# Neighbour maxima over a sparse adjacency: the mask is transposed by DMA instead of by TensorE, and the work of a group is spread differently over its steps

## The chip, the cores and the metric

One core of a Trainium2 chip runs the whole program. The metric is the device time of one execution in microseconds (us), lower is better.

## What is computed

```python
# x: (8, 1024, 128) f32; adj: (8, 1024, 1024) int32, sparse; W: (256, 128); b: (128,)
h = maximum(layernorm(x), 0)
mask = adj != 0
idx = the first 25 set columns of each row of mask      # top_k of -column
agg = max over those neighbours of h[idx]               # and 0, where a row has <= 25
out = x + relu(concat([h, agg], -1) @ W + b)
```

## The kernel before

The 8 × 1024 rows are worked in 16 groups of 512 rows, two groups to a batch. A step of the loop handles one group g and, interleaved with it, prepares group g + 1 and g + 2. Columns are held in 8 classes k (column modulo 8), 128 columns on the partitions. For one group the work is:

- **Mask.** `load_adj` (L221) brings 512 rows of int32. Four signs, one for 128 rows each, make `mask` in bf16 (VectorE `make_mask` L636 for the first two groups, ScalarE `make_mask` L339 after that). `turn_mask` (L449) transposes it on TensorE, 8 blocks of 128×128 in each of 4 turns, into the two-bank PSUM ring, and ScalarE copies each turn to `mask_t` (`turned_mask`, L333).
- **Ranks.** `lower_sums` (L463, 8 matmuls) starts the running counts in the PSUM bank `side`. Then for k = 0 to 7: `prefix_sums` (L469, one matmul) finishes class k in `side`, ScalarE's `find_past` (L349) reads how far past 25 it is, and TensorE's `ranks` (L455, two matmuls) and ScalarE's `stage` (L344) give the rank of every neighbour. `prefix_sums` k waits for `find_past` k − 1.
- **Late neighbours.** `find_late` (L354) marks neighbours above rank 4 of their column block. Seven SyncE DMAs shift the marks by partition (`skew_late`, L233 and L235), `late_ranks` (L455, one or two matmuls a class) and `count` (L491, 8 narrow matmuls) rank them anew, and VectorE's `count_rounds` reads the count.
- **Picks.** A one-hot `hot` (L659, VectorE) times the features, in a high and a low part, fetches neighbours: a **use** is one `pick_pair` (four matmuls, L506 and L507) into one of two PSUM pairs, and one VectorE maximum, `take_pair` (L678). A group has 16 uses, 0 to 15. Uses 0 to 3 run at the end of the step before; ScalarE's `first_maxima` (L378) copies uses 0 and 1 out. Use n may start when take n − 2 has ended. After use 15 come R **late rounds** (R is 1 to 4, 42 in all), each two picks of eight matmuls, two maxima (L775) and two `late_hot` (L684).
- **End.** Two folding maxima (L782, L784), `project` on TensorE (L532, L534, L538) and `finish_group` on VectorE (L691). Group g ends while uses 0 to 3 of group g + 1 run.

The order is written out by hand. Three lists say with which use the preparatory matmuls are issued, right behind its picks, and ScalarE follows the same lists:

```python
LATE_WITH, PREFIX_WITH, RANK_WITH = spread_over(5, 8), spread_over(5, 12), spread_over(9, 13)
LATE_HOT_USES, COUNT_USE, MASK_USES = (10, 11), 9, (4, 9)
```

`LATE_WITH` and `PREFIX_WITH` give the uses of `late_ranks` and `prefix_sums`, `RANK_WITH` that of `ranks`; `count` follows the last `late_ranks`. `COUNT_USE` is the take behind which VectorE reads the count. `lower_sums` runs behind use 4.

New features are normalised once in two steps (odd steps): statistics on VectorE in uses 4 to 8, two passes on GpSimd (`normalize`), the two relu parts on ScalarE (`relu_parts`), the low part on GpSimd, then 14 shifting DMAs on SyncE (`skew_h`). In the start, before the loop, all of this runs once for batch 0, and the masks of groups 0 and 1 are made and turned.

## Time and profile before

| | |
|---|---|
| time, median of 3 runs | 699.37 us (698.42 to 699.73) |
| the profiled execution, its own time | 697.45 us |
| its span | 695.7 us |
| granted TensorE clock, mean | 0.993 |
| TensorE busy | 630.9 us, 91% of the span |
| VectorE busy | 613.7 us, 88% |
| ScalarE busy | 472.3 us, 68% |
| GpSimd busy | 50.3 us, 7% |
| DMA, share of 16 engines | 25.7% |
| VectorE waiting for picks before L678 | 36.0 us, 50 times |

Busy time of TensorE is the modelled length of matmuls that overlap in its pipeline (380 ns each where they start 216 ns apart), so a stretch of it is read from the starts in the timeline. A row of the timeline gives the start and length of an instruction (merged where equal ones follow, with xN), and in brackets how long its engine had been idle before it, and who ended that.

### The profile page before, as it was taken

What the parts mean: (1) busy time and instruction counts of PE and PEld (TensorE: products, weight loads), DVE (VectorE), ACT (ScalarE), POOL (GpSimd) and SP (SyncE); (2) the same over time, 40 slices, a digit from 0 to 9 for tenths busy, and PEclk for the clock granted to TensorE, in tenths of its full rate; (3) what the DMA queues carried; (4) which work ended last, traced back from release to release, by engine and by line L of the source; (5) the groups of instructions that cost most, each with busy time, mean ns of one, the idle gap of its engine ahead of it and who ended that gap; (6) DMA issues with size and microseconds to landing.
All of it is one profiled execution on the core that took longest, in us unless ns stands there. A gap on an engine that the chain in (4) does not pass through costs nothing.

```text
span 695.7 us, 10819 instructions
## 1 busy us (share of the span) xinstructions
PE 630.9 (91%) x3376; PEld 297.4 (43%) x3376; DVE 613.7 (88%) x813; ACT 472.3 (68%) x642; POOL 50.3 (7%) x41
## 2 busy tenths in 40 slices
PE   2479998999989999899999999899999999999976
PEld 2133443535445354443545344353535335353423
DVE  3368999899998999989998899989998899988997
ACT  2689478783777639775795947777497927959120
POOL 1300021000210002100030002100021000300000
PEclk9899999999999999999999999999999999999999
DMA  9520141510415103251303313151122411020100
GB/s 361 199 87 27 60 152 68 182 70 16 152 73 200 60 15 136 83 188 60 128 23 122 151 60 151 68 196 57 41 122 87 185 60 32 16 107 1 60 15 16
DMA packets 19127, 67.64 MB, mean 97 GB/s; under 512 B 4499, under 2 KB 7830, under 8 KB 16534
## 3 DMA queue, kind: packets, MB, share of 16 engines
q1 hardware_dynamic: 19094, 67.26, 25.7%
q8 instruction: 13, 0.21, 0.1%
q14 instruction: 20, 0.16, 0.1%
HBM read 42.08 MB, written 4.19 MB: 67 GB/s over the span
## 4 chain that ended last, share of the span: by engine, by line
PE 66%; DVE 16%; issue 10%; ACT 4%; DVEq 1%; DMA 1%; POOL 1%; ACTq 0%
PE picked L506 18%; PE picked L507 17%; PE ring L455 14%; DVE late_hot L684 4%; PE side L469 4%; PE ring L449 4%; DVE hot L659 4%; PE side L463 4%; DVE best L775 3%; DVE best L678 3%; PE final L534 2%; PE final L538 2%; PE final L491 1%; DMA adj_in<-in_adj_dram 1%; DVEq L771 1%
## 5 line engine op out<-in xcount | busy, mean ns | idle before, releaser
L678 DVE TENSOR_TENSOR best<-picked,best 128x1024 f32<-128x1024 f32 x224 | 270.5, 1218 | 38.2 <-PE picked L507 36.0
L506 PE MATMUL picked<-hot,h_hi 128*128 128x512 f16 x512 | 194.5, 380 | 15.0 <-DVE best L775 7.5
L507 PE MATMUL picked<-hot,h_lo 128*128 128x512 f16 x512 | 194.0, 379 | 0.0
L506 PE MATMUL picked<-late_hot,hi_skew 128*128 128x512 f16 x336 | 127.6, 380 | 13.1 <-DVE late_hot L684 8.2
L507 PE MATMUL picked<-late_hot,lo_skew 128*128 128x512 f16 x336 | 127.3, 379 | 0.0
L344 ACT ACTIVATE late_rank<-ring,late_bias 128x512 bf16<-128x512 f32 x128 | 81.4, 690 | 57.6 <-PE ring L455 57.6
L775 DVE TENSOR_TENSOR best<-picked,best 128x1024 f32<-128x1024 f32 x84 | 102.4, 1219 | 8.3 <-PE picked L507 8.2
L378 ACT COPY best<-picked 128x1024 f32<-128x1024 f32 x32 | 32.2, 1013 | 102.6 <-PE picked L507 102.6
L659 DVE TENSOR_SCALAR hot<-rank 128x4096 f16<-128x4096 bf16 x64 | 89.4, 1399 | 12.0 <-ACT rank L344 12.0
L349 ACT ACTIVATE past<-side,bias_cut 128x512 bf16<-128x512 f32 x128 | 88.3, 690 | 6.2 <-PE side L469 4.9
L344 ACT ACTIVATE rank<-ring,bias_big 128x512 bf16<-128x512 f32 x128 | 83.1, 692 | 5.2 <-PE ring L455 4.9
L684 DVE TENSOR_SCALAR late_hot<-late_rank,numbers 128x2048 f16<-128x2048 bf16 x116 | 86.1, 742 | 0.0
L506 PEld LDWEIGHTS picked<-hot,h_hi 128*128 128x128 f16 x512 | 50.1, 98 | 83.6 <-DVE best L775 14.9
L507 PEld LDWEIGHTS picked<-hot,h_lo 128*128 128x128 f16 x512 | 50.1, 98 | 48.4
L354 ACT ACTIVATE late<-rank,bias_late 128x1024 bf16<-128x1024 bf16 x64 | 68.2, 1137 | 0.0
L333 ACT ACTIVATE mask_t<-ring 128x1024 bf16<-128x1024 bf16 x64 | 62.2, 1023 | 4.8 <-PE ring L449 4.8
L506 PEld LDWEIGHTS picked<-late_hot,hi_skew 128*128 128x128 f16 x336 | 32.6, 97 | 72.0 <-DVE best L775 20.4
L339 ACT ACTIVATE mask<-adj_in 128x1024 bf16<-128x1024 int32 x56 | 57.4, 1050 | 2.8 <-issue 2.8
L469 PE MATMUL side<-mask_t,eye 128*128 128x512 bf16 x128 | 49.5, 387 | 9.4 <-ACT past L349 9.4
L449 PE MATMUL ring<-eye,mask 128*128 128x128 bf16 x512 | 41.0, 231 | 15.0 <-DVE mask L636 11.2
L309 POOL TENSOR_TENSOR h<-x_in,moments 128x1024 f32<-128x1024 f32 x8 | 15.6, 1949 | 500.7 <-DVE gain L655 500.7
L449 PEld LDWEIGHTS ring<-eye,mask 128*128 128x128 bf16 x512 | 40.1, 148 | 24.0 <-issue 11.5
(76 smaller groups left out, 562.1 us busy)
## 6 DMA issues: line engine op xcount, KB each, us to landing
adj_in<-in_adj_dram SPq DMA_DIRECT2D x16, 2048.0 KB, 7.7
late_skew<-late SPq DMA_DIRECT2D x32, 192.0 KB, 2.3
x_in<-in_x_dram SPq DMA_DIRECT2D x8, 512.0 KB, 8.5
xres<-in_x_dram SPq DMA_DIRECT2D x16, 256.0 KB, 7.8
late_skew<-late SPq DMA_DIRECT2D x16, 256.0 KB, 2.4
late_skew<-late SPq DMA_DIRECT2D x32, 128.0 KB, 2.0
out_dram<-xres SPq DMA_DIRECT2D x16, 256.0 KB, 2.0
late_skew<-late SPq DMA_DIRECT2D x32, 64.0 KB, 1.9
```

Source lines behind the costliest of these rows:

```text
L344: nc.scalar.activation(dst[:, k, :], ring[k % 2][:, :], ACT.Relu, bias=bias).then_inc(ring_read, 1)
L349: nc.scalar.activation(past[:, k, :], side[:, :], ACT.Relu, bias=bias_cut[:, 0:1]).then_inc(past_made, 1)
L354: nc.scalar.activation(late[:, 2 * p:2 * p + 2, :], rank[:, s, 2 * p:2 * p + 2, :], ACT.Sign, bias=bias_late[:, 0:1]).then_inc(late_made, 1)
L449: last = nc.tensor.transpose(ring16[n % 2][:, j, q * P:(q + 1) * P], mask[:, q, 2 * n + j::K], eye[:, :])
L455: last = nc.tensor.matmul(ring[k % 2][:, :], w[:, :], m, start=(i == 0), stop=(i == len(terms) - 1))
L469: nc.tensor.matmul(side[:, :], eye[:, :], mask_t[:, k, :], start=False, stop=True, skip_group_check=True).then_inc(prefix_written, 1)
L506: nc.tensor.matmul(dst, hi[:, slot, k, :], onehot, start=start, stop=False)
L507: return nc.tensor.matmul(dst, lo[:, slot, k, :], onehot, start=False, stop=stop)
L659: nc.vector.tensor_scalar(hot[:, (t - 1) % 3, :, :], rank[:, s, :, :], float(t), None, ALU.is_equal).then_inc(hot_made, 1)
L678: nc.vector.tensor_tensor(best[:, half, s, :, :], picked[s][:, :, :], best[:, half, s, :, :], ALU.max).then_inc(picked_read, 1)
L684: nc.vector.tensor_scalar(late_hot[:, part, :], late_rank[:, part, :], which, None, ALU.is_equal).then_inc(late_hot_made[i], 1)
L775: nc.vector.tensor_tensor(best[:, s, i, :, :], picked[i][:, :, :], best[:, s, i, :, :], ALU.max).then_inc(late_read[i], 1)
```

## The change

- **Mask.** The four signs of a group move to the end of a step on ScalarE, behind `first_maxima` (`make_masks`, changed L363), for group g + 3. They read the int32 rows with a step of 8 elements and write `mask` class by class. SyncE issues four DMA transposes a group (`turn_masks`, changed L257) into `mask_t`, which now has two halves. TensorE's 32 transposes and ScalarE's four copies of a group are gone.
- **Order on TensorE.** `lower_sums` for group g + 2 is issued behind `project`, ahead of use 4. The lists change: late ranks with uses 4 to 9, prefix sums with 4 to 11, ranks with 9 to 14. `count` follows use 9, VectorE reads it behind take 11, and makes the late one-hots behind takes 12 and 13.
- **Start.** The features load first and the first mask in four quarters with a semaphore each. VectorE makes only group 0's mask, and both relu parts and the low part of batch 0 (`first_parts`). ScalarE makes the masks of groups 1 and 2; those of group 1 stand ahead of `turned_h`, `find_late` and `first_maxima`. GpSimd's first normalisation waits for group 0's masks.

```diff
-    LATE_WITH, PREFIX_WITH, RANK_WITH = spread_over(5, 8), spread_over(5, 12), spread_over(9, 13)
-    LATE_HOT_USES, COUNT_USE, MASK_USES = (10, 11), 9, (4, 9)
+    LATE_WITH, PREFIX_WITH, RANK_WITH = spread_over(4, 9), spread_over(4, 11), spread_over(9, 14)
+    LATE_HOT_USES, COUNT_USE = (12, 13), 11
...
-        mask = sb("mask", [P, Q, N], BF16)
-        mask_t = sb("mask_t", [P, K, ROWS], BF16)
+        mask = sb("mask", [P, Q, K, P], BF16)
+        mask_t = sb("mask_t", [P, 2, K, ROWS], BF16)
...
+            def turn_masks(slot):
+                sp.reg_add(masks_due, masks_due, Q)
+                for q in range(Q):
+                    sp.wait_ge(mask_made, q + 1)
+                    if q == 0:
+                        sp.wait_ge(mask_made, masks_due)
+                    sp.dma_start_transpose(mask_t[:, slot, :, q * P:(q + 1) * P],
+                                           mask[:, q, :, :].rearrange("p k j -> p (k j)")).then_inc(mask_turned, 16)
...
             load_x(0)
+            for q in range(Q):
+                sp.dma_start(adj_in[:, 0, q * N:(q + 1) * N], adj_v[0][:, q * N:(q + 1) * N]).then_inc(adj_first[q], 16)
             load_adj(1, 1)
...
+            load_adj(2, 0)
+            turn_masks(1)
+            load_adj(3, 1)
             skew_h(0, 0)
             skew_late(0)
+            turn_masks(0)
             def step(it, u):
...
                         skew_h(batch_of(it, u + 1), ((u + 1) // PER_BATCH) % 2)
+                if not at_end(it, u, 3):
+                    turn_masks((u + 1) % 2)
                 sp.wait_ge(result_made, g + 2)
...
+            def make_masks(slot):
+                act.reg_add(turned_due, turned_due, TURNED)
+                act.reg_add(adj_due[slot], adj_due[slot], 16)
+                act.wait_ge(mask_turned, TURNED)
+                act.wait_ge(mask_turned, turned_due)
+                act.wait_ge(adj_loaded[slot], adj_due[slot])
+                for q in range(Q):
+                    counts = adj_in[:, slot, q * N:(q + 1) * N].bitcast(U32).rearrange("p (j k) -> p k j", k=K)
+                    nc.scalar.activation(mask[:, q, :, :], counts, ACT.Sign).then_inc(mask_made, 1)
...
-            stage(TURNS, K - 1, rank[:, 0], bias_big[:, 0:1])
+            stage(0, K - 1, rank[:, 0], bias_big[:, 0:1])
+            make_masks(1)
             turned_h(0, 0)
...
-                if not at_end(it, u, 2):
-                    for n in range(TURNS):
-                        turned_mask(at + TURN_AT, n)
+                if not at_end(it, u, 3):
+                    make_masks((u + 1) % 2)
...
-                    if use == PAIRS and more:
-                        lower_sums(at - TURNS)
...
-                if not at_end(it, u, 2):
-                    turn_mask(g + 2, at + TURN_AT, 0)
                 if more:
                     pick_pair(g + 1, 2, next_slot)
-                if not at_end(it, u, 2):
-                    turn_mask(g + 2, at + TURN_AT, 1)
-                if more:
-                    pick_pair(g + 1, 3, next_slot)
-                if not at_end(it, u, 2):
-                    turn_mask(g + 2, at + TURN_AT, 2)
-                    turn_mask(g + 2, at + TURN_AT, 3)
-                project(g, it, u, new_batch)
+                    pick_pair(g + 1, 3, next_slot)
+                project(g, it, u, new_batch)
+                if not at_end(it, u, 2):
+                    lower_sums(g + 2, u % 2)
...
+            def first_parts():
+                dve.wait_ge(normed_made, 1)
+                nc.vector.tensor_scalar(h_hi[:, 0, :, :], h32[:, :, :], 0.0, None, ALU.max).then_inc(h_made, 1)
+                dve.wait_ge(h_made, 1)
+                nc.vector.tensor_scalar(h32[:, :, :], h32[:, :, :], 0.0, None, ALU.max).then_inc(h_made, 1)
+                dve.wait_ge(h_made, 2)
+                nc.vector.tensor_tensor(h_lo[:, 0, :, :], h32[:, :, :], h_hi[:, 0, :, :], ALU.subtract).then_inc(lo_made, 1)
```

The order of instructions at the places that matter, as built. `ISA` and `REGISTER_ALU` are semaphore and register work and carry no busy time; line numbers of the change are those of its own file.

TensorE in a step, before, from the second half of `lower_sums` through the picks of use 5 to the late ranks of classes 0 and 1:

```order
L463 MATMUL side<-mask_t,before 128x512 x2
L462 REGISTER_ALU
L463 MATMUL side<-mask_t,before 128x512 x2
L518 REGISTER_ALU
L506 MATMUL picked<-hot,h_hi 128x512
L507 MATMUL picked<-hot,h_lo 128x512
L506 MATMUL picked<-hot,h_hi 128x512
L507 MATMUL picked<-hot,h_lo 128x512
L480 ISA
L455 MATMUL ring<-late_skew,half_w 128x512 x2
L455 MATMUL ring<-late_skew,half_ones 128x512
L469 MATMUL side<-mask_t,eye 128x512
```

And changed, the picks of use 4 and what follows them:

```order
L527 ISA
L515 MATMUL picked<-hot,h_hi 128x512
L516 MATMUL picked<-hot,h_lo 128x512
L515 MATMUL picked<-hot,h_hi 128x512
L516 MATMUL picked<-hot,h_lo 128x512
L489 ISA
L460 ISA
L465 MATMUL ring<-late_skew,half_w 128x512
L460 REGISTER_ALU
L465 MATMUL ring<-late_skew,half_w 128x512
L465 MATMUL ring<-late_skew,half_ones 128x512
L478 MATMUL side<-mask_t,eye 128x512
```

The lower sums (L463) stood behind use 4 and are now ahead of it, and the late ranks and the first prefix sum follow use 4 instead of use 5.

TensorE from `count` (L491) on, before; the ranks begin one use later, behind use 9:

```order
L491 MATMUL final<-late_skew,half_ones 32x512 x8
L468 REGISTER_ALU
L469 MATMUL side<-mask_t,eye 128x512
L518 REGISTER_ALU
L506 MATMUL picked<-hot,h_hi 128x512
L507 MATMUL picked<-hot,h_lo 128x512
L506 MATMUL picked<-hot,h_hi 128x512
L507 MATMUL picked<-hot,h_lo 128x512
L468 REGISTER_ALU
L469 MATMUL side<-mask_t,eye 128x512
L441 REGISTER_ALU
L455 MATMUL ring<-mask_t,rank_w 128x512
```

Changed, the tail of use 9:

```order
L465 MATMUL ring<-late_skew,half_w 128x512
L465 MATMUL ring<-late_skew,half_ones 128x512
L500 MATMUL final<-late_skew,half_ones 32x512 x8
L477 REGISTER_ALU
L478 MATMUL side<-mask_t,eye 128x512
L460 REGISTER_ALU
L465 MATMUL ring<-mask_t,rank_w 128x512
L465 MATMUL ring<-past,minus_w 128x512
L460 REGISTER_ALU
L465 MATMUL ring<-mask_t,rank_w 128x512
L465 MATMUL ring<-past,minus_w 128x512
L527 REGISTER_ALU
```

The count (L500), a prefix sum and the ranks of two classes stood behind two different uses and now stand behind one.

SyncE's queue in the start, before, up to the first of the 14 shifts of `skew_h` (L233, `hi_skew`):

```order
L221 DMA adj_in<-in_adj_dram 128x4096
L227 DMA x_in<-in_x_dram 128x1024
L221 DMA adj_in<-in_adj_dram 128x4096
L250 DMA w_in<-in_L_gnn_W_dram 128x2x128
L252 DMA bias_in<-in_L_gnn_b_dram 1x128 x3
L224 DMA xres<-in_x_dram 128x512
L221 DMA adj_in<-in_adj_dram 128x4096 x2
L233 DMA hi_skew<-h_hi 32x1024
```

Changed:

```order
L227 DMA x_in<-in_x_dram 128x1024
L262 DMA adj_in<-in_adj_dram 128x1024 x4
L221 DMA adj_in<-in_adj_dram 128x4096
L264 DMA w_in<-in_L_gnn_W_dram 128x2x128
L266 DMA bias_in<-in_L_gnn_b_dram 1x128 x3
L224 DMA xres<-in_x_dram 128x512
L271 DMA_TRANSPOSE mask_t<-mask 128x8x128 x4
L221 DMA adj_in<-in_adj_dram 128x4096
L252 REGISTER_ALU
L257 DMA_TRANSPOSE mask_t<-mask 128x8x128 x4
L221 DMA adj_in<-in_adj_dram 128x4096
L233 DMA hi_skew<-h_hi 32x1024
```

Eight transposes and a load now stand ahead of the shifts, four of them behind masks that ScalarE makes.

## Rows read from the trace of the kernel before

**Rows 1.** Groups by line and shape: busy, mean of one | idle before, releaser

```profile
L678 DVE TENSOR_TENSOR best<-picked,best 128x1024 f32<-128x1024 f32 x224 | 270.5, 1218 | 38.2 <-PE picked L507 36.0
...
L339 ACT ACTIVATE mask<-adj_in 128x1024 bf16<-128x1024 int32 x56 | 57.4, 1050 | 2.8 <-issue 2.8
L506 PEld LDWEIGHTS picked<-hot,h_hi 128*128 128x128 f16 x512 | 50.1, 98 | 83.6 <-DVE best L775 14.9 <-DVE best L678 14.7 <-issue 6.5
...
L449 PEld LDWEIGHTS ring<-eye,mask 128*128 128x128 bf16 x512 | 40.1, 148 | 24.0 <-issue 11.5 <-ACT mask_t L333 4.3
```

**Rows 2.** Timeline of VectorE, even steps 0 and 2: start, length, instruction, idle before

```profile
51.24 1.23 DVE L678 TENSOR_TENSOR best<-picked,best 128x1024 f32<-128x1024 f32 x1 [1.37 <-PE picked L507]
...
129.26 1.22 DVE L678 TENSOR_TENSOR best<-picked,best 128x1024 f32<-128x1024 f32 x1 [0.17 <-PE picked L507]
131.85 1.22 DVE L678 TENSOR_TENSOR best<-picked,best 128x1024 f32<-128x1024 f32 x1 [1.37 <-PE picked L507]
...
139.41 1.22 DVE L678 TENSOR_TENSOR best<-picked,best 128x1024 f32<-128x1024 f32 x1 [1.16 <-PE picked L507]
```

**Rows 3.** Timeline of VectorE, odd step 1, the same columns

```profile
92.65 1.22 DVE L678 TENSOR_TENSOR best<-picked,best 128x1024 f32<-128x1024 f32 x1 [0.59 <-PE picked L507]
...
100.42 1.23 DVE L678 TENSOR_TENSOR best<-picked,best 128x1024 f32<-128x1024 f32 x1 [0.39 <-PE picked L507]
101.56 0.68 DVE L664 TENSOR_REDUCE late_most<-final 128x1 f32<-128x512 f32 x1
...
103.08 1.23 DVE L678 TENSOR_TENSOR best<-picked,best 128x1024 f32<-128x1024 f32 x1
```

**Rows 4.** Timeline of TensorE around the start of step 2

```profile
124.05 0.38 PE L506 MATMUL picked<-hot,h_hi 128*128 128x512 f16 x1
...
125.99 0.39 PE L532 MATMUL final<-bias_parts,ones 3*128 3x512 bf16 x1
...
128.19 0.38 PE L506 MATMUL picked<-hot,h_hi 128*128 128x512 f16 x1
...
130.78 0.38 PE L506 MATMUL picked<-hot,h_hi 128*128 128x512 f16 x1
...
137.57 0.62 PE L491 MATMUL final<-late_skew,half_ones 128*32 128x512 bf16 x8
...
140.38 0.38 PE L506 MATMUL picked<-hot,h_hi 128*128 128x512 f16 x1
```

**Rows 5.** Timeline of ScalarE, end of step 1 and start of step 2

```profile
122.39 1.01 ACT L378 COPY best<-picked 128x1024 f32<-128x1024 f32 x1 [0.53 <-PE picked L507]
...
132.06 1.26 ACT L344 ACTIVATE late_rank<-ring,late_bias 128x512 bf16<-128x512 f32 x2 [3.58 <-PE ring L455]
```

**Rows 6.** Timeline of all engines in the start

```profile
8.55 2.50 DVE L636 TENSOR_SCALAR mask<-adj_in 128x1024 bf16<-128x1024 int32 x4 [7.47 <-DMA adj_in<-in_adj_dram]
...
16.48 2.38 PE L463 MATMUL side<-mask_t,before 128*128 128x512 bf16 x8
...
26.56 0.67 ACT L349 ACTIVATE past<-side,bias_cut 128x512 bf16<-128x512 f32 x1
...
36.12 1.49 ACT L344 ACTIVATE rank<-ring,bias_big 128x512 bf16<-128x512 f32 x2
```

**Rows 7.** Timeline of SyncE's queue: the start, then the end of step 1

```profile
26.68 1.16 SPq L233 DMA_DIRECT2D hi_skew<-h_hi  x2
...
34.90 0.59 SPq L235 DMA_DIRECT2D lo_skew<-h_lo  x1
...
128.20 0.59 SPq L235 DMA_DIRECT2D lo_skew<-h_lo  x1
...
152.22 1.11 SPq L233 DMA_DIRECT2D late_skew<-late  x2
```

**Rows 8.** DMA issues of the page: KB each, median us to landing

```profile
adj_in<-in_adj_dram SPq DMA_DIRECT2D x16, 2048.0 KB, 7.7
...
late_skew<-late SPq DMA_DIRECT2D x16, 256.0 KB, 2.4
```

More of the change, by code:

```diff
@@ L61, in build @@
     SKEWS = 16 * (2 * CHAINS - 1)
[L64 to L67 removed]
+    FIRST_RING = K
+    RING = 2 * K
+    LATE_AT, RANK_AT = 0, K
+    TURNED = 16 * Q
     assert C == P and K == 8 and PER_BATCH == 2 and BASE == 4
@@ L307, in normalize @@
                 pool.wait_ge(gain_made, 2 * batch + 2)
+                if isinstance(batch, int) and batch == 0:
+                    pool.wait_ge(mask_made, Q)
                 mean = moments[:, :, 0:1].to_broadcast([P, K, C])
@@ L378, in first_maxima @@
                 nc.scalar.copy(best[:, half, s, :, :], picked[s][:, :, :]).then_inc(picked_copied, 1)
-            for n in range(TURNS):
-                turned_mask(0, n)
+            turned_due = act.alloc_register("act_turned_due")
+            adj_due = [act.alloc_register(f"act_adj_due{s}") for s in range(2)]
+            for due in (turned_due, *adj_due):
+                act.reg_mov(due, 0)
             spreads(0)
-            relu_parts(0, 0)
             for k in range(K):
@@ L394, in _ @@
             for p in range(1, PAIRS):
-                find_late(p, 0, FIRST_RING - TURNS)
-            for n in range(TURNS):
-                turned_mask(FIRST_RING - TURNS, n)
+                find_late(p, 0, FIRST_RING)
+            make_masks(0)
             def step(it, u):
@@ L405, in step @@
                 for use in range(PAIRS, USES):
-                    if use in MASK_USES and not at_end(it, u, 2):
-                        make_mask(MASK_USES.index(use), u % 2, 16 * (it * (UNROLL // 2) + u // 2 + 2), at)
                     for k in LATE_WITH[use]:
@@ L441, in take @@
                     pe.wait_ge(ring_read, at - 1)
-            def turn_mask(g, at, n):
-                if n == 0:
-                    pe.wait_ge(mask_made, Q * (g + 1))
-                take(at + n)
-                for j in range(2):
-                    for q in range(Q):
-                        last = nc.tensor.transpose(ring16[n % 2][:, j, q * P:(q + 1) * P], mask[:, q, 2 * n + j::K], eye[:, :])
-                last.then_inc(ring_written, 1)
             def accumulate(at, k, terms):
@@ L545, in _ @@
             pe.wait_ge(basics_made, 10)
-            for n in range(TURNS):
-                turn_mask(0, 0, n)
             pe.wait_ge(basics_made, 13)
-            lower_sums(0)
+            lower_sums(0, 0)
             pe.wait_ge(consts_made, 5)
             for k in range(K):
-                prefix_sums(0, k)
+                prefix_sums(0, 0, k)
                 if k:
-                    ranks(0, TURNS, k - 1)
-            ranks(0, TURNS, K - 1)
+                    ranks(0, 0, 0, k - 1)
+            ranks(0, 0, 0, K - 1)
             turn_h(0, True)
@@ L559, in _ @@
                 pick_pair(0, use, 0)
-            for n in range(TURNS):
-                turn_mask(1, FIRST_RING - TURNS, n)
+            lower_sums(1, 1)
             pe.wait_ge(h_turned, 2)
@@ L698, in _ @@
                 nc.vector.memset(held[:, i:i + 1], 0.0).then_inc(opened, 1)
-            for q in range(Q):
-                make_mask(q, 0, 16, None)
             stats_of(0, range(K))
             moments_of(0)
+            first_mask(0)
+            make_gain(0)
+            for q in range(1, Q):
+                first_mask(q)
             dve.wait_ge(basics_made, 13)
```

78 lines of the change are left out of this document (31 added, 47 removed).

## Prediction

> **What bounds the kernel now.** The page's busy shares put TensorE (91%) and VectorE (88%) close together, so an average decides nothing: which of the two waits changes within a step. I read next the groups by line. VectorE's take of a pick, L678, is its largest work and waits 36.0 us in all for picks [rows 1]; nearly all idle time of VectorE after the start is there. The timelines show where. In an even step it waits before take 4 (0.17), take 5 (1.37) and take 9 (1.16) [rows 2]; in an odd step, where the statistics for the next batch keep it busy, before take 5 (0.59) and take 9 (0.39) [rows 3]. On the other side TensorE goes without a gap from the picks of use 4 at 128.19 to those of use 10 at 140.38 [rows 4]. So uses 4 to 9 are TensorE's, and from take 9 to the end of the step VectorE paces: late rounds, folding, one-hots, finish. TensorE's work pays only where it stands between a take and its pick in uses 4 to 10. ScalarE, at 68%, has its copies of uses 0 and 1 done at 123.40 (122.39 + 1.01) and stages the first late rank at 132.06 [rows 5]. In the start the ranks' chain begins with `find_past` at 26.56 and ends at 37.6 [rows 6].
>
> **The units.** In rows 4, 130.78 − 128.19 = 2.59 us holds 12 matmuls (picks of use 4, lower sums): 0.216 each, 0.86 a use. A take starts 1.07 after its picks do (128.19 and 129.26, 130.78 and 131.85) [rows 2, 4]; takes in a row start 1.14 apart, and the reading of the count puts 1.52 between two takes (101.56 to 103.08) [rows 3].
>
> **Transposes out of TensorE.** 32 transposes a group stand between the picks of uses 1, 2, 3 and `project`. Without them the picks of use 3 no longer start at 124.05 but when ScalarE's second copy ends, about 123.5, and end at 124.5; `project` (125.99 to 128.19, 2.20) [rows 4] ends at 126.7 instead of 128.19. VectorE finishes its own chain of that stretch (fold, one-hots, takes 2 and 3) only around 128.2, as now, so this 1.5 us is a lead of TensorE, no gain yet.
>
> **Lower sums behind the projection.** They take 8 × 0.216 = 1.73 and end at 128.4. The picks of use 4 start 0.24 later than now, take 4 at 129.5. Behind them stand three late-rank matmuls and a prefix sum, 0.86, so the picks of use 5 start at 130.15 and take 5 at 131.2, where it is 131.85 now: 0.6 won.
>
> **The new spread, even steps.** From the end of `project` to the picks of use 10 TensorE now needs 140.38 − 128.19 = 12.19 [rows 4]. The change leaves all of that in, since the lower sums, all late ranks, the count and the ranks of two classes are still ahead of use 10, and adds one more prefix sum (0.22). It also adds waits for `find_past`: use 4 sends ScalarE two stages (1.26) [rows 5] and a `find_past` of 0.69, done at about 131.6, while use 5 brings only one late matmul, so the second prefix sum, due at 131.2, waits 0.4; the same behind uses 7 and 8. So it is 126.7 + 12.19 + 0.22 + 0.74 = 139.85 for the picks of use 10. Take 10 starts at 140.9, take 11 after two more matmul groups (0.86 + 0.65) at 142.4. Now take 9 starts at 139.41, and the second take behind it would, the count aside, start at 139.41 + 2 × 1.14 = 141.7 [rows 2, 3]. The difference is **+0.74 us** a step. The reason is the cover: now VectorE reads the count for 1.5 us just while TensorE does use 9's ranks. In the change a late rank of two matmuls, the count, a prefix sum and four rank matmuls (7 × 0.216 + 0.6 [rows 4] = 2.1) stand behind use 9 in one lump, and VectorE has only takes to do until take 11.
>
> **Odd steps.** The statistics hide the lower sums already: of its waits of 0.59 and 0.39 [rows 3] VectorE loses about 0.45 and 0.39, so take 9 starts at 99.6 instead of 100.42 and take 7 ends at 98.0. The picks of use 9 must wait for that, since a use waits for the take two before it. They need 0.86 and a restart of 0.17, then the lump: picks of use 10 at 101.25, take 10 at 102.3, take 11 at 103.8, against 100.42 + 2.28 = 102.7 now. **+1.1 us**. Seven even steps (2 to 14) and seven odd ones (1 to 13): 5.2 + 7.7 = 12.9. In step 0 the part from take 5 on costs 142.4 − 131.2 against 141.7 − 131.85 (step 2 stands for it), +1.4.
>
> **ScalarE's signs.** 56 of 1.05 us [rows 1] become 60, all in the step's last quarter; the 64 copies from PSUM go. Four signs back to back behind the copy end at 127.3, and the first late rank reaches ScalarE at 129.7, so they cost nothing as long as one takes under 1.6 us. What they read has a step of 32 bytes, which no ScalarE row shows. The cheap end is 1.05. The nearest strided row is TensorE's weight load from the mask at a step of 16 bytes, 148 ns [rows 1], half as long again as the 98 ns of a dense load, L506 [rows 1]: 1.6. I take 1.05 and keep 1.6 for the range.
>
> **DMA transposes in the loop.** Per group four, 1 MB in all. SyncE issues them behind its last shift; it is free from 128.2 and next has something urgent at 152.2 [rows 7], so up to some 20 us stay covered. Uncovered is the start.
>
> **The start.** Features and the first mask are 2.5 MB where the mask alone is 2 MB and lands in 7.7 [rows 8]; the last quarter lands at about 9.9, VectorE's sign is 0.63 (2.50 for four) [rows 6], so masks are made at 10.6. The transposes stand in the queue behind the 2 MB of group 1 and land at about 16.5. With 2.4 for the lower sums, `find_past` starts at 19.2 instead of 26.56, because ScalarE no longer waits for GpSimd's normalisation. The chain of 11 us (26.56 to 37.6) [rows 6] ends at 30.3, **7.3 us earlier**. Then it is given back. ScalarE signs group 1 first (3.9, to 34.2). SyncE waits for these masks, issues four transposes, and behind them 14 feature shifts and 7 late shifts, which now start at 26.68 at 0.63 each [rows 7], long before the late marks. Price of a transpose in the queue: no row shows one. The cheap end is a shift's 0.63, the dear end a 256 KB shift served alone, 2.4 [rows 8]; I take 1.2, nearer the cheap end because issue and not bytes sets the pace of the shifts. So 34.2 + 4.8 + 0.4, + 21 × 0.63 = 52.6, landed at 54.3; late ranks and a prefix sum 0.86, take 5 1.07 later at 56.2, now 51.24 [rows 2]. **+5.0 us**. VectorE's three new parts run inside the chain of ranks and cost nothing; if the chain got shorter than 8 us they would show.
>
> The Trainium skill (Advanced Engine Details and Errata, X-Bar Transpose) states that transposing DMAs on this chip are as fast as regular ones. By that the four would cost 0.63 each and the sum would be 2.3 us lower; no row here shows it.
>
> **Sum.** 697.45 + 12.9 + 1.4 + 5.0 = 716.75, say **717 us**. The profiled execution was 1.9 us below the median of the runs shown, 699.37, so by the median it would be 719; I stay with 717. Within this case the time lies between 705 (half of the steps' cost, transposes at 0.63 and not queued) and 726 (2.4 each, signs 1.6).
>
> **Rivals.**
>
> - *Faster: the relief of TensorE goes through.* If TensorE is ahead by about 2 us at use 9, the lump is covered and the waits for the lower sums go: 7 × (1.37 + 0.59) = 13.7, and the 7.3 of the start are kept: 676.4. For it speaks that 2 us a group leave the fuller engine. Against it, TensorE has no gap from 128.19 to 140.38, and a use can't start before the take two earlier has ended, so it can't get that far ahead. It decides at take 10.
> - *Slower still: signs with a step.* At twice 1.05 four signs end at 131.6; late ranks come to ScalarE at 129.7 and TensorE's third one at 131.0 waits for the first to be staged, 1.1 us a step or 16 in all, and 4.2 in the start: 737. Nothing in a ScalarE row speaks for it; the 148 ns speak for some slowing. The Trainium skill (SBUF — State Buffer, Door 1: The DMA port swizzle, the note on cachelines) says that accesses which each fall in a new 16-byte line pay a penalty, and a step of 32 bytes does that; it gives no figure.
> - *Transposes that are dear.* At 7.7 us each, the time of the 2 MB load [rows 8], the start pays 26 us more, 743 or above, and the 20 us of cover in the loop are used up.
> - *Nothing to see.* Start and steps cancel, 697: it takes a start 7 us earlier and steps 0.5 dearer each.
>
> **How the numbers follow.** Forecast 0.58, faster 0.20, strided signs 0.12, dear transposes 0.06, nothing 0.04. A measurement of this kernel tells 0.2% (1.4 us) from no change. Slower is 0.76, the same 0.04, faster 0.20. The range takes in the forecast's 705 to 726, and the strided case above, and below it holds the case of no change and reaches into the faster case, whose own spread is about 670 to 697: 692 to 742.
>
> **What would show it.** Right: a wait of 1.5 to 2 us before take 10 in every step and some 0.4 before take 11, none worth naming before take 5 in odd steps; groups 0.7 to 1.1 us longer from finish to finish; TensorE in step 0 waiting some 10 us for the late shifts behind use 4; signs near 1.05. Wrong: steps as long as before or shorter would mean that the lump is covered; signs over 1.6, or late ranks waiting for ScalarE, the second rival; `skew_late` late in the loop, the third.

## The result, and the profile after

| | before | changed |
|---|---|---|
| time, median of 4 runs | 698.89 us (697.42 to 699.73) | 744.11 us (741.07 to 748.99) |
| the profiled execution, its own time | 697.45 us | 743.42 us |
| its span | 695.7 us | 740.6 us |
| granted TensorE clock, mean | 0.993 | 0.973 |
| TensorE busy | 630.9 us | 615.6 us |
| VectorE waiting for picks before its take | 36.0 us, 50 times | 84.9 us, 88 times |

The ratio is 1.066, 95% interval 1.060 to 1.072: slower by 45 us, where the forecast said 19. The direction was right, the size was not, and 744 lies above the range (692 to 742).

Groups by line of the changed kernel, as in [rows 1]:

```profile
L683 DVE TENSOR_TENSOR best<-picked,best 128x1024 f32<-128x1024 f32 x224 | 270.9, 1218 | 86.0 <-PE picked L516 84.9
...
L363 ACT ACTIVATE mask<-adj_in 128x1024 bf16<-128x1024 uint32 x60 | 119.7, 2071 | 0.6 <-DMA mask_t<-mask 0.6
...
L465 PE MATMUL ring<-late_skew,half_w 128*128 128x512 bf16 x128 | 44.1, 386 | 19.6 <-ACT late_rank L368 10.6
L472 PE MATMUL side<-mask_t,before 128*128 128x512 bf16 x128 | 33.3, 407 | 22.6 <-DMA mask_t<-mask 22.6
```

TensorE was relieved (15.3 us less busy) and VectorE has the same work, but waits 49 us more. One sign takes 2071 ns, twice the 1050 of [rows 1], and late ranks (L465) now wait for ScalarE.

Where the 44.9 us of span lie is read from the finishes of groups (the rows of `xres` in VectorE's timeline). The first finish comes at 106.89 instead of 89.32, **17.6 us** later. From the first finish to the last it is 630.6 us instead of 603.2, **27.3 us** more: an odd step with two late rounds takes 40.9 instead of 39.1, an even one with four 47.1 instead of 45.3, and three odd steps are another 0.9 to 1.3 longer.

An even step, VectorE's timeline after the finish at 147.79, takes 4, 5, 6, 9, 10 and 11; it answers to [rows 2]:

```profile
147.79 0.68 DVE L696 SCALAR_TENSOR_TENSOR xres<-final,xres 128x512 f32<-128x512 f32 x1
148.98 1.22 DVE L683 TENSOR_TENSOR best<-picked,best 128x1024 f32<-128x1024 f32 x1 [0.51 <-PE picked L516]
150.71 1.22 DVE L683 TENSOR_TENSOR best<-picked,best 128x1024 f32<-128x1024 f32 x1 [0.50 <-PE picked L516]
...
153.92 1.23 DVE L683 TENSOR_TENSOR best<-picked,best 128x1024 f32<-128x1024 f32 x1 [0.85 <-PE picked L516]
...
158.84 1.23 DVE L683 TENSOR_TENSOR best<-picked,best 128x1024 f32<-128x1024 f32 x1 [0.45 <-PE picked L516]
161.86 1.22 DVE L683 TENSOR_TENSOR best<-picked,best 128x1024 f32<-128x1024 f32 x1 [1.80 <-PE picked L516]
163.37 1.23 DVE L683 TENSOR_TENSOR best<-picked,best 128x1024 f32<-128x1024 f32 x1 [0.29 <-PE picked L516]
```

The wait of 1.80 before take 10 and that of 0.29 before take 11 are the forecast's lump. The waits before take 4 (0.51) and take 6 (0.85) are not in it. That before take 4 goes with the lower sums' new place ahead of use 4: it is 0.51 in every version that has them there, also with short signs (experiment 6) and with the old lists (experiment 3). That before take 6 comes from ScalarE; its timeline and TensorE's in the same step:

```profile
142.86 7.99 ACT L363 ACTIVATE mask<-adj_in 128x1024 bf16<-128x1024 uint32 x4
150.76 1.24 ACT L368 ACTIVATE late_rank<-ring,late_bias 128x512 bf16<-128x512 f32 x2
151.90 0.68 ACT L373 ACTIVATE past<-side,bias_cut 128x512 bf16<-128x512 f32 x1
...
151.48 0.39 PE L465 MATMUL ring<-late_skew,half_w 128*128 128x512 bf16 x1 [0.81 <-ACT late_rank L368]
152.63 0.39 PE L478 MATMUL side<-mask_t,eye 128*128 128x512 bf16 x1 [0.76 <-ACT past L373]
```

ScalarE goes from its fourth sign (ends at 150.85) into the late ranks without a gap, so it was late for them, and TensorE waits twice.

The start, SyncE's queue, and the engines that it waits for or keeps waiting; it answers to [rows 6] and [rows 7]:

```profile
8.33 11.29 SPq L271 DMA_TRANSPOSE mask_t<-mask  x4
...
43.26 5.38 SPq L257 DMA_TRANSPOSE mask_t<-mask  x4
48.68 0.58 SPq L221 DMA_DIRECT2D adj_in<-in_adj_dram  x1
49.31 1.17 SPq L233 DMA_DIRECT2D hi_skew<-h_hi  x2
...
58.23 1.23 SPq L233 DMA_DIRECT2D late_skew<-late  x2
...
62.06 0.59 SPq L235 DMA_DIRECT2D late_skew<-late  x1
...
21.63 3.26 PE L472 MATMUL side<-mask_t,before 128*128 128x512 bf16 x8 [21.63 <-DMA mask_t<-mask]
...
25.15 0.69 ACT L373 ACTIVATE past<-side,bias_cut 128x512 bf16<-128x512 f32 x1 [18.25 <-PE side L478]
...
35.31 7.87 ACT L363 ACTIVATE mask<-adj_in 128x1024 bf16<-128x1024 uint32 x4
...
64.58 1.03 PE L465 MATMUL ring<-late_skew,half_w 128*128 128x512 bf16 x2 [8.92 <-DMA late_skew<-late]
...
68.21 1.22 DVE L683 TENSOR_TENSOR best<-picked,best 128x1024 f32<-128x1024 f32 x1 [11.29 <-PE picked L516]
```

It is the chain of the forecast (ranks, masks of group 1, transposes, 21 shifts, late ranks), each link longer: take 5 starts at 68.21, forecast 56.2, before 51.24 [rows 2].

### The profile page after: what moved, and what is told of

Read it like the earlier page. It is cut to its first block, busy times and chain, and to the rows that moved or that the text cites. A ratio compares the mean times of both kernels' runs of the same rounds, so it can differ in the third digit from the quotient of the medians.

```text
span 740.6 us, 9651 instructions
## 1 busy us (share of the span) xinstructions
PE 615.6 (83%) x2864; PEld 265.3 (36%) x2864; DVE 613.5 (83%) x812; ACT 480.2 (65%) x579; POOL 47.5 (6%) x40
## 2 busy tenths in 40 slices
DMA packets 87139, 84.36 MB, mean 114 GB/s; under 512 B 72131, under 2 KB 75462, under 8 KB 84678
## 4 chain that ended last, share of the span: by engine, by line
PE 31%; DVE 23%; ACT 19%; issue 17%; SPq 2%; DVEq 1%; ACTq 0%; DMA 0%
ACT mask L363 12%; PE picked L515 11%; PE picked L516 10%; DVE late_hot L689 6%; DVE best L683 6%; PE ring L465 5%; DVE best L780 3%; DVE hot L664 3%; PE side L478 3%; ACT late_rank L368 3%; ACT past L373 2%; DVE late_most L669 1%; PE final L500 1%; DVE late_other L672 1%; SPq L233 1%
## 5 line engine op out<-in xcount | busy, mean ns | idle before, releaser
L683 DVE TENSOR_TENSOR best<-picked,best 128x1024 f32<-128x1024 f32 x224 | 270.9, 1218 | 86.0 <-PE picked L516 84.9
L515 PE MATMUL picked<-hot,h_hi 128*128 128x512 f16 x512 | 196.6, 384 | 33.3 <-DVE best L683 13.4
L515 PE MATMUL picked<-late_hot,hi_skew 128*128 128x512 f16 x336 | 129.6, 386 | 17.2 <-DVE late_hot L689 8.4
L516 PE MATMUL picked<-late_hot,lo_skew 128*128 128x512 f16 x336 | 128.9, 384 | 0.0
L363 ACT ACTIVATE mask<-adj_in 128x1024 bf16<-128x1024 uint32 x60 | 119.7, 2071 | 0.6 <-DMA mask_t<-mask 0.6
L368 ACT ACTIVATE late_rank<-ring,late_bias 128x512 bf16<-128x512 f32 x128 | 84.6, 686 | 39.8 <-PE ring L465 39.3
L465 PE MATMUL ring<-late_skew,half_w 128*128 128x512 bf16 x128 | 44.1, 386 | 19.6 <-ACT late_rank L368 10.6
L472 PE MATMUL side<-mask_t,before 128*128 128x512 bf16 x128 | 33.3, 407 | 22.6 <-DMA mask_t<-mask 22.6
L465 PE MATMUL ring<-mask_t,rank_w 128*128 128x512 bf16 x128 | 48.5, 379 | 0.3 <-ACT past L373 0.3
```

The source lines that it names most:

```text
L363: nc.scalar.activation(mask[:, q, :, :], counts, ACT.Sign).then_inc(mask_made, 1)
L368: nc.scalar.activation(dst[:, k, :], ring[k % 2][:, :], ACT.Relu, bias=bias).then_inc(ring_read, 1)
L465: last = nc.tensor.matmul(ring[k % 2][:, :], w[:, :], m, start=(i == 0), stop=(i == len(terms) - 1))
L515: nc.tensor.matmul(dst, hi[:, slot, k, :], onehot, start=start, stop=False)
L516: return nc.tensor.matmul(dst, lo[:, slot, k, :], onehot, start=False, stop=stop)
L683: nc.vector.tensor_tensor(best[:, half, s, :, :], picked[s][:, :, :], best[:, half, s, :, :], ALU.max).then_inc(picked_read, 1)
```

## The experiments

Three theories. **Lump**: the new lists put late rank, count, prefix sum and four rank matmuls between two picks. **Signs**: reading a row with a step doubles them, and ScalarE is late. **Queue**: the start pays what SyncE has ahead of the late shifts. A version that was timed only once is judged by its steps and finishes, read from its own trace.

**1. The prices by themselves.** A small kernel of signs and transposes with nothing beside them; here the read with a step of 8 and the stepped write:

```python
nc.scalar.activation(step8[:, i, :, :], c.rearrange("p (j k) -> p k j", k=8), ACT.Sign)
nc.scalar.activation(spread8[:, i, :, :].rearrange("p k j -> p j k"),
                     c.rearrange("p (j k) -> p j k", k=8), ACT.Sign)
```

> A kernel for prices alone: it computes nothing of the reference but copies x to the output. ScalarE signs 1024 int32 a row four times in each of: dense, read with a step of 2, 4 and 8 elements, and dense read with a write step of 128 elements; then bf16 read with a step of 8. VectorE does dense, read step 8 and write step 128. Then one DMA transpose of 256 KB alone and four in a row, with nothing beside them. Theory 'the step': the sign of the change costs 2.07 us because every element read lies in a new 16 byte line, so steps of 2 (8 bytes, two elements a line) cost about the dense 1.04, steps of 4 and 8 elements about 2.07, and bf16 at a step of 8 (16 bytes) about 2.07 as well. Rival 'the neighbours': the sign is slowed by what runs beside it (TensorE's picks, the transposing DMAs); then it costs about 1.04 at every step here. The transposes: by 'the step' nothing; if the queue's pace of 1.35 us each seen in the change is their own cost, it is 1.3 to 1.4 here too, and if it comes from loads ahead of them it is near 0.6.

Its groups by line: dense (L99), read with a step of 2 (L101), 4 (L103) and 8 elements (L105), written with a step of 128 elements (L107), bf16 read with a step of 8 (L111); the same on VectorE, dense, read by 8, written by 128 (L120, L122, L125):

```profile
L107 ACT ACTIVATE spread<-counts 128x1024 bf16<-128x1024 int32 x4 | 18.3, 4956 | 0.0
L125 DVE TENSOR_SCALAR v_spread<-counts 128x1024 bf16<-128x1024 int32 x4 | 9.3, 2634 | 0.0
L105 ACT ACTIVATE step<-counts 128x1024 bf16<-128x1024 int32 x4 | 7.8, 2018 | 0.0
L111 ACT ACTIVATE half<-half 128x1024 bf16<-128x1024 bf16 x4 | 7.7, 2002 | 0.0
L103 ACT ACTIVATE step<-counts 128x1024 bf16<-128x1024 int32 x4 | 7.7, 1984 | 0.0
L101 ACT ACTIVATE step<-counts 128x1024 bf16<-128x1024 int32 x4 | 4.1, 1091 | 0.0
L122 DVE TENSOR_SCALAR v_step<-counts 128x1024 bf16<-128x1024 int32 x4 | 4.0, 1068 | 0.0
L99 ACT ACTIVATE dense<-counts 128x1024 bf16<-128x1024 int32 x4 | 3.9, 1044 | 3.9 <-DMA counts<-in_adj_dram 3.9
L120 DVE TENSOR_SCALAR v_dense<-counts 128x1024 bf16<-128x1024 int32 x4 | 2.5, 689 | 48.0 <-ACT half L111 48.0
```

The step is the whole price of the sign, and it comes in one jump: 1044 and 1091 up to 8 bytes, 1984 from 16 bytes on. That agrees with the Trainium skill (SBUF — State Buffer, Door 1, the note on cachelines), which wants at least two hits on each 16-byte line and gives no figure for the penalty. Its list of free steps, 4 elements of fp32 and 8 of bf16, doesn't hold for ScalarE here: 4 elements of int32 cost 1984 ns and 8 of bf16 2002. Four transposes alone took 5.37 us of the queue, 1.34 each, so their pace in the change (5.38) is their own.

**2. Step on the other side**, dense reads and stepped writes:

```diff
-  counts = adj_in[...].bitcast(U32).rearrange("p (j k) -> p k j", k=K)
-  nc.scalar.activation(mask[:, q, :, :], counts, ACT.Sign)
+  counts = adj_in[...].rearrange("p (j k) -> p j k", k=K)
+  nc.scalar.activation(mask[:, q, :, :].rearrange("p k j -> p j k"), counts, ACT.Sign)
```

> The change, with ScalarE's signs reading the int32 rows densely and writing bf16 with a step of 128 elements (256 bytes), so that the mask in memory is the same. Theory 'the sign': if writing with a step is free, a sign takes about 1.05 us, the late ranks no longer wait for ScalarE, and the run is what the prediction assumed, 715 to 722 us, with steps of about 40.3 (two late rounds, odd) and 46 (four rounds, even). If writing costs as reading does, 2.07 and 744. Rival 'the transposes': their 68000 small packets slow the steps; then the time stays above 735 even if the sign takes 1.05.

A miss: a sign took 4995 ns, the whole 918.54 us, and TensorE waited 146.5 us for `late_rank`. Not a way out, but it shows what long signs do: they push the late ranks.

**3. The change with the lists of before.**

```diff
-  ... = spread_over(4, 9), spread_over(4, 11), spread_over(9, 14)
-  LATE_HOT_USES, COUNT_USE = (12, 13), 11
+  ... = spread_over(5, 8), spread_over(5, 12), spread_over(9, 13)
+  LATE_HOT_USES, COUNT_USE = (10, 11), 9
```

> The change, with the lists of the kernel before: late ranks with uses 5 to 8, prefix sums with 5 to 12, ranks with 9 to 13, count read behind take 9, late one-hots behind takes 10 and 11. Theory 'the lump': the wait of 1.8 us before take 10 goes, steps fall to about 39.0 (odd, two rounds) and 44.8 (even, four rounds), 700 to 706 us in all, though signs still take 2.07. It also takes most of the signs' harm away, since the first late rank comes a use later. Rival 'the signs and the queue': the steps are longer because ScalarE is late and SyncE is late; the lists matter little, 738 to 745.

702.80 us (before on that chip 697.59). Steps 38.6 and 44.25: each **0.5 and 1.1 us shorter than before**, though the signs are as long. The first finish is at 105.84, so the start stays. Hence the lists cost some 41 us in the changed kernel, and without them the relief of TensorE does go through. The 41 us hold much of what the long signs cost too, since with the old lists the first late rank comes a use later: TensorE's waits for `late_rank` fall from 10.6 to 2.0 us in all. The small packets of the DMA transposes (72131 under 512 bytes against 4499 before) are all still there, so they are not what lengthens the steps.

**4. Only the reading of the count back behind take 9.**

```diff
-  LATE_HOT_USES, COUNT_USE = (12, 13), 11
+  LATE_HOT_USES, COUNT_USE = (12, 13), 9
```

> The change, with one number other: VectorE reads the count behind take 9 instead of take 11. Theory 'the cover': the 1.5 us of reading then run beside the lump on TensorE, the wait before take 10 falls from 1.8 to under 1 us, each step is about 0.6 to 0.8 shorter, 730 to 734 us. Rival: the count's matmuls stand behind the picks of use 9 and VectorE now waits for them before it can take 10; nothing is won, 742 to 746.

730.09 us, steps 40.4 and 45.95. VectorE's timeline, even step:

```profile
159.55 1.22 DVE L683 TENSOR_TENSOR best<-picked,best 128x1024 f32<-128x1024 f32 x1 [0.45 <-PE picked L516]
160.69 0.68 DVE L669 TENSOR_REDUCE late_most<-final 128x1 f32<-128x512 f32 x1
...
162.58 1.23 DVE L683 TENSOR_TENSOR best<-picked,best 128x1024 f32<-128x1024 f32 x1 [0.33 <-PE picked L516]
```

The wait before take 10 falls from 1.80 to 0.33: the count covers the lump, as the forecast had it. But only 1.1 us of an even step come back, and 0.5 of an odd one. In the odd step TensorE now waits 1.95 us for ScalarE's `h` instead of 1.45, and the other waits for picks stay.

**5. The new lists in the kernel before.**

```diff
-  ... = spread_over(5, 8), spread_over(5, 12), spread_over(9, 13)
-  LATE_HOT_USES, COUNT_USE, MASK_USES = (10, 11), 9, (4, 9)
+  ... = spread_over(4, 9), spread_over(4, 11), spread_over(9, 14)
+  LATE_HOT_USES, COUNT_USE, MASK_USES = (12, 13), 11, (4, 9)
```

> The kernel before with the change's lists alone (late ranks with uses 4 to 9, prefix sums with 4 to 11, ranks with 9 to 14, count read behind take 11, late one-hots behind 12 and 13); masks still dense and turned on TensorE. Theory 'the lists cost by the lump behind use 9, whatever else is changed': steps of 41 to 42 (odd) and 47 to 48 us (even) instead of 39.1 and 45.3, a wait of 1.5 to 2.5 before take 10, 720 to 732 in all, the first finish within 2 us of 89.3. Rival 'the lists cost only together with the new place of signs and lower sums': 697 to 705.

735.98 us, above the range of 720 to 732, steps 41.25 and 47.18, the same 1.80 before take 10 of an even step. One step took 52.7, with TensorE idle for 3.62 at 221.9 and nothing that released it, so the kernel was run again:

> The same kernel as in the earlier run of the kernel before with the change's lists, now timed in rounds, since that look held one wait of 3.6 us of TensorE that nothing explains and a clock dip behind it. Theory 'the wait was an accident of that execution': steps of 41.3 and 47.2 us throughout, with some odd steps 1.4 us longer from a clock dip, 722 to 732 in all. Rival 'the lists bring that wait about': it comes again in the profiled execution, and 733 or more.

735.32 us (ratio 1.051, interval 1.049 to 1.052). The wait was no accident; it came at the same instruction again:

```profile
221.63 1.06 PE L538 MATMUL final<-w_scaled,agg_t 128*128 128x128 f32 x8
226.65 0.60 PE L506 MATMUL picked<-hot,h_hi 128*128 128x512 f16 x1 [3.96 <-issue]
...
221.60 2.85 SPq L233 DMA_DIRECT2D lo_skew<-h_lo  x1
```

SyncE's issue of 0.59 us takes 2.85 at the same moment, so something that both engines need may have been held up. What, the trace doesn't show. The place is where TensorE's code, a loop of four steps, jumps back to its head for the first time; neither the kernel before nor the changed one waits there. It costs some 6 us of the 36, once a program. The other 30 are the lists: the first finish 2.9 to 3.7 later, and 14 steps at about 2.

**6. Dense signs under the new lists.** Only the stretch from a finish to its later takes is compared.

```diff
-  counts = adj_in[...].bitcast(U32).rearrange("p (j k) -> p k j", k=K)
+  counts = adj_in[...].bitcast(U32).rearrange("p (k j) -> p k j", k=K)
```

> The change with one edit: ScalarE's signs read the int32 row densely instead of with a step of 8, so the masks of groups 1 to 15 hold the columns in another order and the neighbours and the rounds of those groups are others (total time and whole steps are not to be compared; the stretch from a group's finish to its take 10 and the start before take 5 are). One sign should last 1.05 us instead of 2.07, four 4.2 instead of 8.0. Theory 'strided signs delay the late ranks': the wait of TensorE for late_rank (0.81 and 0.76 in the change) goes and the stretch from finish to take 10 gets shorter by about 0.8 us in even and odd steps. Rival 'the signs are covered in the loop': that stretch stays within 0.2 us. In the start both expect take 5 about 4 us earlier, near 64 instead of 68.2.

Four signs end 2.44 us before ScalarE is wanted, and TensorE's waits for `late_rank` and `past` behind use 5 go:

```profile
143.21 3.90 ACT L363 ACTIVATE mask<-adj_in 128x1024 bf16<-128x1024 uint32 x4
149.54 1.27 ACT L368 ACTIVATE late_rank<-ring,late_bias 128x512 bf16<-128x512 f32 x2 [2.44 <-PE ring L465]
...
160.68 1.23 DVE L683 TENSOR_TENSOR best<-picked,best 128x1024 f32<-128x1024 f32 x1 [1.80 <-PE picked L516]
```

The wait of 1.80 before take 10 stays. From a group's finish to the start of take 14, a point behind lump, count and late one-hots in every version (the second finish for the even, the first for the odd step):

| | even step | odd step |
|---|---|---|
| before | 19.82 | 19.91 |
| changed | 21.83 (+2.01) | 21.84 (+1.93) |
| changed, dense signs | 20.30 (+0.48) | 20.95 (+1.04) |
| changed, old lists | 18.98 (−0.84) | 19.59 (−0.32) |
| before, new lists | 21.70 (+1.88) | 22.05 (+2.14) |

With dense signs the loss is 0.48 and 1.04; the forecast, which took them at 1.05 us, had 0.74 and 1.1. So the step in the signs costs 1.5 and 0.9 a step under these lists. In the start take 5 comes at 64.68, 3.5 us earlier, close to the expected 64.

**7. The start: SyncE's order alone.**

```diff
+            skew_h(0, 0)
             turn_masks(1)
             load_adj(3, 1)
-            skew_h(0, 0)
             skew_late(0)
```

> The change with one edit in SyncE's queue of the start: the 14 shifts of the features stand ahead of the transposes of group 1 (and behind the load of group 2) instead of behind them. Nothing else is moved, ScalarE still makes group 1's masks. Theory 'feature shifts wait in the queue behind transposes whose masks come late': the 14 shifts, 9 us of queue, go under the chain of ranks; take 5 and the first finish come 5 to 8 us earlier, near 100 instead of 106.9, steps unchanged, 735 to 740 in all. Rival 'the late shifts wait for their marks and for the engines, not for the queue': first finish within 2 us of 106.9.

A miss: the late shifts are issued at 50.49 to 54.82, 8 us earlier, but land only at 61.2. They take 6.7 to 7.7 us from issue to landing, where the median is 1.9 to 2.4. What stands close ahead of them now is the 2 MB load of group 3, which itself takes 9.3 us; that it is the cause was not tried by itself:

```profile
49.01 0.58 SPq L221 DMA_DIRECT2D adj_in<-in_adj_dram  x1
50.49 1.10 SPq L233 DMA_DIRECT2D late_skew<-late  x2
...
61.20 1.03 PE L465 MATMUL ring<-late_skew,half_w 128*128 128x512 bf16 x2 [7.57 <-DMA late_skew<-late]
```

The first finish is 104.34, 2.5 us won. The time, 744.15, is no better, because six steps came out 1.4 us longer, against three in the change. TensorE's timeline in such a step (here the change's, 218 to 223) shows what they are:

```profile
218.68 0.85 PE L510 MATMUL side<-eye,h 128*128 128x128 f32 x4 [1.45 <-ACT h L389]
219.33 1.06 PE L510 MATMUL final<-eye,h 128*128 128x128 f32 x4
220.18 0.63 PE L515 MATMUL picked<-late_hot,hi_skew 128*128 128x512 f16 x1
220.61 0.63 PE L516 MATMUL picked<-late_hot,lo_skew 128*128 128x512 f16 x1
...
222.59 0.38 PE L515 MATMUL picked<-late_hot,hi_skew 128*128 128x512 f16 x1
```

After a wait of 1.45 us for ScalarE's `h` the matmuls of one picking start 0.43 apart instead of 0.216, the granted clock in that stretch is 0.5 (1.2 GHz), and it is back at full after some 3 us. In stretches of 2 us between 88 and 640 us the change has five with a clock below 0.95 and this run eleven. The four kernels with the old lists wait 0.89 us there and show none. But the wait alone doesn't decide: experiment 8's kernel waits 1.45 us in all seven odd steps that work on new features, and shows no dip either. What else it takes is open.

**8. Group 1's masks on VectorE**, under ScalarE's chain of ranks:

```diff
-            make_masks(1)
...
+            def second_masks():
+                dve.wait_ge(mask_turned, TURNED)
+                dve.wait_ge(adj_loaded[1], 16)
+                for q in range(Q):
+                    nc.vector.tensor_scalar(mask[:, q, :, :], adj_in[:, 1, q * N:(q + 1) * N].rearrange("p (j k) -> p k j", k=K),
+                                            0.0, None, ALU.not_equal).then_inc(mask_made, 1)
...
+            second_masks()
```

The removed line is ScalarE's, the added call stands behind `first_parts()`.

> The change with group 1's masks made by VectorE right behind its three first parts, while ScalarE runs the chain of ranks of group 0, instead of by ScalarE behind that chain. Theory 'the start is one queue: masks of group 1, their transposes, the shifts, the late shifts': the masks (7.9 us on ScalarE), most of the transposes and part of the shifts move under the chain; take 5 comes 10 to 15 us earlier, the first finish near 92 instead of 106.9, the steps stay at 40.9 and 47.1 us, 729 to 734 in all. Rival 'the start waits for bytes, not for the masks' (loads and 64 KB transposes compete in the DMA engines): the first finish moves by less than 4 us, above 740.

726.33 us, first finish 93.16: 13.7 us of the start are back, as the queue theory says. The steps are those of the change, but for its three clock dips, which did not come; that is another 4 us and why the time lies below the 729 to 734 expected.

**9 to 11. Putting it together.** All keep the change's DMA transposes. The first takes the old lists, masks of group 1 on VectorE, and on SyncE in the start the first transposes ahead of group 1's load and `skew_h` ahead of `turn_masks(1)`. The second also puts one of the four signs ahead of `first_maxima`. The third also has new lists:

```diff
-            load_adj(1, 1)
-            load_xres(0, 0)
...
+            load_adj(1, 1)
             load_adj(2, 0)
+            load_xres(0, 0)
+            skew_h(0, 0)
             turn_masks(1)
             load_adj(3, 1)
-            skew_h(0, 0)
...
+                    make_masks((u + 1) % 2, range(0, 1))
                 if more:
                     for s in range(2):
                         first_maxima(g + 1, s, (u + 1) % 2)
                 if not at_end(it, u, 3):
-                    make_masks((u + 1) % 2)
+                    make_masks((u + 1) % 2, range(1, Q))
...
-  ... = spread_over(5, 8), spread_over(5, 12), spread_over(9, 13)
+  ... = spread_over(4, 7), spread_over(4, 11), spread_over(9, 12)
```

> The change's relief of TensorE with the lists of before, group 1's masks made by VectorE under the chain of ranks, and SyncE's queue in the start in the order first transposes, load of group 1's rest, shifts of the features, transposes of group 1. Theory (steps 38.6 and 44.25 as in the run with the old lists, start given back by its queue alone): first finish near 88 to 92, 684 to 690 in all, faster than both. Rival 'the start cannot be had back': first finish above 100, 697 or more.

> The former best version with one of a group's four signs moved ahead of ScalarE's two copies of uses 0 and 1, where ScalarE has 4.6 us idle in an odd step. Three signs (6 us) are left behind the copies. Theory 'the strided signs still hold up the late ranks in even steps': TensorE's wait for late_rank and VectorE's wait of about 1.1 before take 6 shrink, even steps 43 to 43.9 instead of 44.25, odd steps 38.3 to 38.6, 672 to 677 in all instead of 681.5. Rival 'signs are covered with these lists': 680 to 683.

> The version of best2 with lists worked out anew: late ranks with uses 4 to 7, prefix sums with 4 to 11, ranks with 9 to 12, count read behind take 9, late one-hots behind 10 and 11. The count then stands behind use 7 and no longer beside the first ranks: no stretch between two picks holds more than a prefix sum and four rank matmuls. Theory 'what costs is the lump on TensorE': odd steps about 37.3 to 38, even 43.5 to 44.3, 665 to 675 in all. Rival 'VectorE and late ranks pace now': within 2 us of best2, or slower since the late ranks come too early for ScalarE's signs.

| | time, us | ratio to before | first finish | steps, odd and even |
|---|---|---|---|---|
| first | 681.52 | 0.974 (0.973 to 0.976) | 85.96 | 38.6, 44.25 |
| second | 678.53 | 0.971 (0.969 to 0.973) | 86.08 | 38.6, 43.6 |
| third | 670.49 | 0.960 (0.958 to 0.961) | 87.49 | 36.9, 44.05 |

The first beat its range of 684 to 690. With the loads of group 1 and of `xres` behind them the first four transposes take 5.94 us of the queue instead of 11.29, and the lower sums start at 16.17 instead of 21.63. The third version's timelines, start and an odd step:

```profile
8.16 5.94 SPq L269 DMA_TRANSPOSE mask_t<-mask  x4
...
16.17 3.57 PE L475 MATMUL side<-mask_t,before 128*128 128x512 bf16 x8 [16.17 <-DMA mask_t<-mask]
...
107.29 2.14 POOL L325 TENSOR_TENSOR h_lo<-h,h_hi 128x1024 f16<-128x1024 f32 x1 [5.37 <-ACT h L390]
...
108.80 1.72 DVE L674 TENSOR_SCALAR hot<-rank 128x4096 f16<-128x4096 bf16 x1
```

And the same one-hot in the second version:

```profile
107.95 2.88 DVE L674 TENSOR_SCALAR hot<-rank 128x4096 f16<-128x4096 bf16 x1
```

The second, with 6 us of signs behind the copies instead of 8, gains 0.65 in an even step and nothing in an odd one. The steps are as expected, but 678.5 lies between the 672 to 677 of the theory and the 680 to 683 of its rival. In the third, odd steps gain 1.7 and even ones lose 0.45. The time lies in the lump theory's range, but does not bear it out: 1.16 of the 1.7 is a one-hot of 1.72 us instead of 2.88, told at the end, and seven times that is 8.1 us, all that the third version gains over the second (8.0). What the odd steps gain besides, the even steps and the start (1.4 us later) lose again.

## Why the prediction was right or wrong

- **The lump** (0.74 and 1.1 a step): right as mechanism and, with dense signs, near in size (0.48 and 1.04). Waits of 1.80 and 0.29 stood where 1.5 to 2 and 0.4 were foretold. That lists alone slow the kernel before by 30 us and more shows how much of VectorE's pace hangs on the lists. One sum of the forecast slips: 98.0 + 0.86 + 0.17 + 2.1 makes 101.1 for the picks of use 10 in an odd step, not 101.25, and so 1.0 instead of 1.1.
- **"I take 1.05 and keep 1.6 for the range"**: this step failed. A sign measured 2.07. The weight load on TensorE was the wrong row to bound it by: its step was 16 bytes too, but another engine's reading says little of ScalarE's. Four signs take 8.0 us, past the point from which the text said they would cost (1.6 each). It is the rival of signs with a step, to which 0.12 was given; it priced 1.1 us a step, the runs show 1.5 and 0.9, and its 737 lies 6 below the 743.42 of the profiled execution. Of the 26.7 us that the forecast lacks there (743.42 against 716.75), the signs are 16.9 in the steps and 4.0 in the start.
- **The start** (+5.0 at take 5; measured +17.0): the chain was right, its links were short. The transposes of group 0 landed at 21.6, not 16.5 (+5.1): the first two took 4.55 and 3.96 us of the queue, while the loads of group 1 and of `xres` ahead of them were still landing (at about 15.9 and 17.1), and the last two 1.31 and 1.33; masks of group 1 took 7.87, not 3.9 (+4.0); transposes 1.35 each, not 1.2, and a load's issue of 0.58 was left out (+0.9 with what lies between); late ranks and picks up to take 5 took 3.6 us at half clock, not 1.9 (+1.7). That is 11.7 of the 12.0 missing. By the Trainium skill (Advanced Engine Details and Errata, X-Bar Transpose) transposes are as fast as regular DMAs; here one takes 1.35 us of the queue against 0.63 for a shift, and alone it lands 3.1 us after its issue against 2.4 for a shift of the same 256 KB. VectorE's masks were taken at 0.63 too, without their step, and took 1.08 each, ready at 12.1 instead of 10.6; the queue hid that. From take 5 to the first finish step 0 cost 0.6 us, where 1.4 was forecast.
- **Transposes in the loop cost nothing**: right. `turn_masks` ran at 110.04 for 5.71 us in the step after 106.89, and no engine waited for a transposed mask after the start.
- **The sum of steps** (12.9, measured 27.3): over steps 1 to 14 the lump is 10.6 of it (0.48 and 1.04, seven steps each), the signs' step 16.9 (1.53 and 0.89), and three clock dips 3.2, which the forecast didn't have. Behind take 14 VectorE waits less than before, which gives back 0.3 and 0.1 a step (2.5). Step 14 has nothing to sign and is 0.5 longer instead of 1.8, step 12 is 1.5 longer (together 1.5 less), and the last step, 15, adds 0.6. That makes 27.3.
- **Rival "the relief goes through"** (676.4): fell with these lists, at take 10 as foretold. With the old ones it lives: steps of 38.6 and 44.25, which are 0.5 and 1.1 shorter than before, and 681.5 us once the start is mended. Its objection that TensorE can't get ahead past use 9 was true of the lists and not of the relief.

Open: what held TensorE and SyncE for 4 us in the kernel before with new lists; what else than the wait of 1.45 us brings a clock dip; and what dense signs would be worth under the old lists, which no run tried.

## What to carry to other kernels

Price an instruction whose access pattern changes by its own engine with that pattern, even if it takes a small kernel to get the number: a step of 16 bytes doubled it, and everything on the engine behind it moved. Relief of the fuller engine pays only if the order that was tuned to the old load is kept or worked out again; a bundle of relief and new order has to be tried apart. In a start that is one chain, put each queue's late-wanted loads behind the transfers that the chain waits for.

## What was not expected of the hardware

- A read step of 16 bytes or more takes ScalarE from 1044 to about 2000 ns for 1024 elements, int32 or bf16 alike; a write step of 256 bytes takes it to 4956. VectorE takes 689 dense, 1068 with a read step of 32 bytes and 2634 with that write step.
- A DMA transpose of a 128×1024 bf16 block takes 1.34 us of SyncE's queue alone, and took 4.55 and 3.96 while a load of 2 MB and one of 256 KB issued ahead of it were still landing.
- VectorE's one-hot (1.22 us) is held while GpSimd's low part runs. Before the change, in the odd step, VectorE's timeline and GpSimd's:

```profile
111.50 2.88 DVE L659 TENSOR_SCALAR hot<-rank 128x4096 f16<-128x4096 bf16 x1
...
111.17 2.13 POOL L303 TENSOR_TENSOR h_lo<-h,h_hi 128x1024 f16<-128x1024 f32 x1 [7.18 <-ACT h L365]
```

The one-hot ends 1.08 us after GpSimd's instruction (113.30), and in the third version too (109.43 and 110.52), where GpSimd was further ahead and the one-hot took 1.72. In all seven odd steps of seven traces (before, changed, experiments 3, 8 and 9 to 11) the one-hot ends 1.07 to 1.10 us after that instruction. In the third version the ranks end a use earlier, so GpSimd's low part starts 19.8 us after the first finish instead of 21.5 in the second. That is 1.2 us an odd step which no list was meant to give.
